# Four score bands in one fill and one 2048-column exponential per half-step

## The reference, cut to what matters

```
x0, x1, x2 = einsum('bnc,c->bn', xf, w1|w2|w3) + b       # n = 4096 positions of one image
sim   = x0[:, :, None] * x1[:, None, :]                  # 4096 x 4096
sm    = softmax(sim, axis=1)
feats = einsum('bn,bnm->bm', x2, sm)
gate  = sigmoid(feats);  layer = gate * x
```

## Time and profile before

| | us |
|---|---|
| median of 3 runs | 5597.88 (5597.68 to 5598.18) |
| the profiled execution, its time | 5609.25 |
| the profiled execution, its span | 5607.3 |
| PE busy | 5256.8 (94%) |
| DVE busy | 4116.6 (73%) |
| ACT busy | 3974.4 (71%) |
| POOL busy | 1925.3 (34%) |

### The profile page before, as it was taken

How to read it: one execution, slowest core, us unless ns; L and a number is a source line. 1 busy time by engine, 2 the same in 40 slices (tenths; PEclk the granted TensorE clock), 3 DMA queues, 4 the chain that set the end, 5 groups by cost and what they waited for, 6 DMA issues and landing times.

```text
span 5607.3 us, 113930 instructions
## 1 busy us (share of the span) xinstructions
PE 5256.8 (94%) x44520; PEld 2738.1 (49%) x44520; DVE 4116.6 (73%) x8686; ACT 3974.4 (71%) x6017; POOL 1925.3 (34%) x1588
## 2 busy tenths in 40 slices
PE   7799999999999999999999999999999999999996
PEld 3436445364553645446364553645446364453624
DVE  8467677777777777677777777777777776777726
ACT  1467868677785877868677785877858678676795
POOL 3224243342423424243341423424234251433403
PEclk9899999999999999999999999999999999999997
DMA  2010201102011020201102011020201102011000
GB/s 85 6 40 11 67 26 50 38 6 72 20 61 31 17 64 14 66 26 39 47 7 71 22 61 31 13 67 14 64 28 32 52 11 67 26 45 41 7 31 31
DMA packets 163252, 211.22 MB, mean 38 GB/s; under 512 B 13216, under 2 KB 146080, under 8 KB 162720
## 3 DMA queue, kind: packets, MB, share of 16 engines
q1 hardware_dynamic: 138144, 136.79, 7.6%
q0 software_dynamic: 24576, 67.14, 4.1%
HBM read 136.78 MB, written 67.11 MB: 36 GB/s over the span
## 4 chain that ended last, share of the span: by engine, by line
PE 67%; ACT 13%; DVE 11%; issue 6%; POOL 2%; DMA 1%; ACTq 0%; DVEq 0%; POOLq 0%; SPq 0%
PE PS L1185 33%; PE PS L1362 15%; PE PS L1353 6%; ACT n_x L510 3%; DVE stats L839 2%; PE PS L1461 2%; PE PS L1219 2%; PE PS L1243 2%; PE PS L1296 2%; ACT xin L510 2%; ACT big L582 2%; ACT work L549 1%; ACT attn L559 1%; ACT soft L582 1%; DMA quant_H<-emb_t,idx 1%
## 5 line engine op out<-in xcount | busy, mean ns | idle before, releaser
L582 ACT ACTIVATE big<-PS 128x1024 f32<-128x1024 f32 x1376 | 1365.8, 1024 | 463.5 <-PE PS L1353 401.8
L582 ACT ACTIVATE soft<-PS 128x1024 f32<-128x1024 f32 x672 | 676.1, 1024 | 352.9 <-PE PS L1353 345.2
L405 POOL DMA_INDIRECT quant_H<-emb_t,idx x512 | 487.5, 952 | 979.9 <-DVE idx L863 788.2
L1185 PE MATMUL PS<-e_hi,n_hi 128*128 128x512 f16 x2048 | 781.4, 382 | 17.5 <-POOL n_lo L398 8.5
L1185 PE MATMUL PS<-e_lo,n_hi 128*128 128x512 f16 x2048 | 778.0, 380 | 0.0
L1185 PE MATMUL PS<-e_hi,n_lo 128*128 128x512 f16 x2048 | 777.8, 380 | 0.0
L1362 PE MATMUL PS<-big,w 128*4 128x512 f32 x5504 | 756.8, 639 | 0.0
L839 DVE BATCH_NORM_STATS2 stats<-XT 128x6 f32<-128x512 f32 x1024 | 651.8, 683 | 14.5 <-POOL XT L421 4.9
L863 DVE FIND_INDEX8 idx<-m,work 128x8 uint32<-128x1024 f32 x512 | 622.1, 1219 | 0.0
L1353 PE MATMUL PS<-rhs,lhs 12*128 12x512 bf16 x4096 | 558.3, 395 | 60.9 <-ACT big L582 38.6
L857 DVE CUSTOM_DVE_ANT_0 work<-PS,e_bias,m 128x512 f32<-128x512 f32 x512 | 384.0, 750 | 211.7 <-PE PS L1185 205.8
(11 more groups left out here) (208 smaller groups left out, 10795.1 us busy)
## 6 DMA issues: line engine op xcount, KB each, us to landing
xin<-x SPq DMA_DIRECT2D x128, 512.0 KB, 3.9
out<-yout SPq DMA_DIRECT2D x128, 512.0 KB, 2.9
quant_H<-emb_t,idx POOLq DMA_INDIRECT x512, 2.7
XT<-emb SPq DMA_DIRECT2D x1, 1024.0 KB, 6.1
XT<-wh SPq DMA_DIRECT2D x1, 256.0 KB, 5.7
XT<-wqv SPq DMA_DIRECT2D x1, 256.0 KB, 5.8
XT<-wk SPq DMA_DIRECT2D x1, 128.0 KB, 5.7
w_sb<-w SPq DMA_DIRECT2D x1, 128.0 KB, 5.3
```

Source lines behind the costliest of these rows:

```text
L405: nc.gpsimd.indirect_dma_start(quant[:, g % 2, u, :], None, emb_t, bass.IndirectOffsetOnAxis(ap=idx[:, t % (2 * GT), 0:1], axis=0),).then_ ...
L582: nc.scalar.activation(E[h % 3][:, z * 1024:(z + 1) * 1024], bank(2 * z, 2), ACT.Exp).then_inc(exped.sem, 1)
L1185: ins = mm(dst, a, b, start=first and j == 0, stop=last and j == 2)
```

## The change

`whole(im, h)` is true for half-steps 1 to 63 of images 0 to 14. There `fill(im, h, 0)` does nothing, and `fill(im, h, 1)` writes all four bands with four matmuls. It waits, as line 1350 has it, until both exponential counts of half-step `h-1` are reached. `exp(im, h, 0)` is then one exponential of 2048 columns, and `exp(im, h, 1)` does nothing. Half-step 0 and the last image keep the old form. The order of the stretch in the 15 rounds of the loop is written anew on POOL, ACT, DVE and PE. The tail and what follows the stretch are the same work in the same order. The calls `prepare(new, ...)` that the new lists hold do nothing for `new` > 0.

The core of the diff, with the new order of PE over the stretch, and of ACT at its beginning and around half-step 32:

```diff
@@ -290,6 +290,9 @@
 
         def z_ps(im, c):
             return bank(0 if im == B - 1 and c % 2 == 1 else 5).rearrange("p (u n) -> p u n", u=2)
+
+        def whole(im, h):
+            return h > 0 and im < B - 1
 
         def back_bank(im, c):
             return 4 if im == B - 1 and c % 2 == 1 else 6
...
             def exp(im, h, z):
-                act.wait_ge(*filled.after(im, 2 * h + z))
+                if whole(im, h):
+                    if z == 1:
+                        return
+                    act.wait_ge(*filled.after(im, 2 * h + 1))
+                else:
+                    act.wait_ge(*filled.after(im, 2 * h + z))
                 if z == 0:
                     act.wait_ge(*summed.room(im, h, 3))
                     if h == 2 and im > 0:
                         act.wait_ge(*l3_ctxed.after(im - 1, NG - 1))
-                nc.scalar.activation(E[h % 3][:, z * 1024:(z + 1) * 1024], bank(2 * z, 2),
-                                     ACT.Exp).then_inc(exped.sem, 1)
+                if whole(im, h):
+                    nc.scalar.activation(E[h % 3], bank(0, 4), ACT.Exp).then_inc(exped.sem, 2)
+                else:
+                    nc.scalar.activation(E[h % 3][:, z * 1024:(z + 1) * 1024], bank(2 * z, 2),
+                                         ACT.Exp).then_inc(exped.sem, 1)
 
...
             def fill(im, h, z):
                 f, t = h // NT, h % NT
+                if whole(im, h) and z == 0:
+                    return
                 if h + z == 0:
                     pe.wait_ge(*pieces_kept[0].after(im, 2))
                     pe.wait_ge(*pieces_kept[1].after(im, 1))
@@ -1348,10 +1362,10 @@
                 if h == 0 and z == 1 and im > 0:
                     pe.wait_ge(*l3_qlo.after(im - 1, NG - 3))
                 pe.wait_ge(*exped.room(im, 2 * h + z, 2))
-                for r in range(2 * z, 2 * z + 2):
+                for r in range(0 if whole(im, h) else 2 * z, 2 * z + 2):
                     rr = slice(32 * r, 32 * r + PIECES)
                     ins = mm(bank(r), lhs[rr, t * P:(t + 1) * P], rhs[rr, f * GW:(f + 1) * GW], start=True, stop=True)
-                ins.then_inc(filled.sem, 1)
+                ins.then_inc(filled.sem, 2 if whole(im, h) else 1)
 
             def sums(im, h):
                 f, t = h // NT, h % NT
@@ -1497,103 +1511,101 @@
             gn(new, 2, 2); project(new); extremes(new); piece_turn(new, 0); piece_turn(new, 1); piece_turn(new, 2)
             piece_turn(new, 3); piece_turn(new, 4)
             for new, old, last in images(B):
-                l3_kturn(last, 7); fill(old, 0, 0); fill(old, 0, 1); fill(old, 1, 0); fill(old, 1, 1)
...
```

New order on ACT (block `scalar`), beginning and half-steps 31 to 36:

```diff
+                exp(old, 0, 0); exp(old, 0, 1); exp(old, 1, 0); exp(old, 1, 1); combine(last, 0); exp(old, 2, 0)
+                exp(old, 2, 1); exp(old, 3, 0); exp(old, 3, 1); l3_qexp(last, 7); exp(old, 4, 0)
+                l3_qturn(last, 6); exp(old, 4, 1); exp(old, 5, 0); final_sq(last, 0); exp(old, 5, 1)
+                exp(old, 6, 0); exp(old, 6, 1); exp(old, 7, 0); exp(old, 7, 1); final_sq(last, 1); exp(old, 8, 0)
+                exp(old, 8, 1); exp(old, 9, 0); l3_qturn(last, 7); final_sq(last, 2); exp(old, 9, 1)
+                exp(old, 10, 0); final_sq(last, 3); exp(old, 10, 1); exp(old, 11, 0); final_sq(last, 4)
...
+                exp(old, 31, 0); exp(old, 31, 1); l0_norm(new, 0, 0); l0_norm(new, 0, 1); l0_norm(new, 0, 2)
+                l0_norm(new, 0, 3); exp(old, 32, 0); l0_norm(new, 1, 0); l0_norm(new, 1, 1); l0_norm(new, 1, 2)
+                exp(old, 32, 1); l0_norm(new, 1, 3); l0_norm(new, 2, 0); l0_norm(new, 2, 1); exp(old, 33, 0)
+                exp(old, 33, 1); exp(old, 34, 0); exp(old, 34, 1); l0_norm(new, 2, 2); l0_norm(new, 2, 3)
+                exp(old, 35, 0); exp(old, 35, 1); exp(old, 36, 0); exp(old, 36, 1); exp(old, 37, 0)
+                l0_norm(new, 3, 0); l0_norm(new, 3, 1); exp(old, 37, 1); exp(old, 38, 0); exp(old, 38, 1)
...
```

New order on PE (block `tensor`), the whole stretch. `fill(old, h, 0)` with `h` > 0 is empty:

```diff
+                fill(old, 0, 0); fill(old, 0, 1); l3_kturn(last, 7); fill(old, 1, 0); fill(old, 1, 1)
+                fill(old, 2, 0); sums(old, 0)
+                l3_ctx(last, 7); fill(old, 2, 1); fill(old, 3, 0); sums(old, 1)
+                fill(old, 3, 1); l3_qturn(last, 6); combine(last, 1); combine(last, 2); fill(old, 4, 0)
+                fill(old, 4, 1); fill(old, 5, 0); sums(old, 2)
+                final_z(last, 0); fill(old, 5, 1); fill(old, 6, 0); sums(old, 3)
+                sums(old, 4)
+                fill(old, 6, 1); fill(old, 7, 0); l3_qturn(last, 7); final_z(last, 1); fill(old, 7, 1)
+                fill(old, 8, 0); final_out(last, 0); sums(old, 5)
+                fill(old, 8, 1); fill(old, 9, 0); final_z(last, 2); fill(old, 9, 1); sums(old, 7)
+                final_out(last, 1); sums(old, 8)
+                fill(old, 10, 0); fill(old, 10, 1); turn_in(new, 0); fill(old, 11, 0); final_z(last, 3)
+                fill(old, 11, 1); sums(old, 9)
+                final_out(last, 2); final_z(last, 4); turn_in(new, 1); fill(old, 12, 0); fill(old, 12, 1)
+                fill(old, 13, 0); final_z(last, 5); sums(old, 10)
+                fill(old, 13, 1); fill(old, 14, 0); final_out(last, 3); turn_in(new, 2); final_z(last, 6)
+                fill(old, 14, 1); sums(old, 11)
+                sums(old, 12)
+                final_z(last, 7); fill(old, 15, 0); turn_in(new, 3); final_out(last, 4); fill(old, 15, 1)
+                fill(old, 16, 0); sums(old, 13)
+                fill(old, 16, 1); final_out(last, 5); fill(old, 17, 0); turn_in(new, 4); sums(old, 14)
+                sums(old, 15)
+                final_out(last, 6); fill(old, 17, 1); turn_in(new, 5); fill(old, 18, 0); final_z(last, 8)
+                prepare(new, 0); fill(old, 18, 1); fill(old, 19, 0); final_out(last, 7); sums(old, 16)
+                final_z(last, 9); sums(old, 17)
+                fill(old, 19, 1); turn_in(new, 6); final_z(last, 10); turn_in(new, 7); fill(old, 20, 0)
+                final_out(last, 8); final_z(last, 11); fill(old, 20, 1); fill(old, 21, 0); final_out(last, 9)
+                turn_in(new, 8); final_z(last, 12); fill(old, 21, 1); fill(old, 22, 0); sums(old, 19)
+                turn_in(new, 9); sums(old, 20)
+                final_out(last, 10); fill(old, 22, 1); sums(old, 21)
+                final_z(last, 13); turn_in(new, 10); final_out(last, 11); fill(old, 23, 0); fill(old, 23, 1)
+                final_z(last, 14); fill(old, 24, 0); fill(old, 24, 1); sums(old, 23)
+                turn_in(new, 11); final_out(last, 12); fill(old, 25, 0); fill(old, 25, 1); fill(old, 26, 0)
+                final_z(last, 15); sums(old, 24)
+                final_out(last, 13); turn_in(new, 12); fill(old, 26, 1); fill(old, 27, 0); sums(old, 25)
+                final_out(last, 14); fill(old, 27, 1); turn_in(new, 13); turn_in(new, 14); fill(old, 28, 0)
+                fill(old, 28, 1); final_out(last, 15); sums(old, 26)
+                fill(old, 29, 0); fill(old, 29, 1); turn_in(new, 15); sums(old, 27)
+                fill(old, 30, 0); fill(old, 30, 1); fill(old, 31, 0); sums(old, 28)
+                gn(new, 0, 1); gn(new, 0, 2); fill(old, 31, 1); fill(old, 32, 0); fill(old, 32, 1); sums(old, 29)
+                score(new, 0, 0); score(new, 0, 1); score(new, 1, 0); score(new, 1, 1); fill(old, 33, 0)
+                fill(old, 33, 1); score(new, 2, 0); fill(old, 34, 0); sums(old, 32)
+                fill(old, 34, 1); score(new, 2, 1); score(new, 3, 0); fill(old, 35, 0); fill(old, 35, 1)
+                sums(old, 33)
+                score(new, 3, 1); score(new, 4, 0); turn0(new, 0); score(new, 4, 1); sums(old, 34)
+                score(new, 5, 0); fill(old, 36, 0); fill(old, 36, 1); score(new, 5, 1); score(new, 6, 0)
+                fill(old, 37, 0); fill(old, 37, 1); sums(old, 35)
+                fill(old, 38, 0); turn0(new, 1); score(new, 6, 1); score(new, 7, 0); fill(old, 38, 1)
+                sums(old, 36)
+                score(new, 7, 1); fill(old, 39, 0); fill(old, 39, 1); fill(old, 40, 0); score(new, 8, 0)
+                score(new, 8, 1); fill(old, 40, 1); sums(old, 37)
+                fill(old, 41, 0); sums(old, 38)
+                turn0(new, 2); sums(old, 39)
+                score(new, 9, 0); score(new, 9, 1); score(new, 10, 0); fill(old, 41, 1); score(new, 10, 1)
+                fill(old, 42, 0); fill(old, 42, 1); fill(old, 43, 0); turn0(new, 3); score(new, 11, 0)
+                fill(old, 43, 1); score(new, 11, 1); score(new, 12, 0); sums(old, 40)
+                score(new, 12, 1); turn0(new, 4); score(new, 13, 0); fill(old, 44, 0); score(new, 13, 1)
+                fill(old, 44, 1); score(new, 14, 0); score(new, 14, 1); turn0(new, 5); fill(old, 45, 0)
+                score(new, 15, 0); score(new, 15, 1); score(new, 16, 0); score(new, 16, 1); score(new, 17, 0)
+                turn0(new, 6); fill(old, 45, 1); sums(old, 42)
+                score(new, 17, 1); sums(old, 44)
```

(69 more changed lines are left out.)

245 lines of the change are left out of this document (91 added, 154 removed).

## The result

The changed kernel took 5874.62 us (median of 4 runs, 5864.6 to 5882.28), the kernel before 5598.03 us beside it. The ratio is 1.0484, with a 95% interval of 1.0472 to 1.0496. It is slower by 277 us, 18.4 us for each of the 15 rounds. The forecast was 5780 us, 12 us a round, and its range ended at 5910. The profiled execution took 5882.28 us.

What follows compares the result with a forecast made beforehand. ACT and PE were taken to bound the first half by turns, PE the second. Lost overlap +8.3 us a round plus 4 of other waits gave +12, 15 rounds 180 us: 5780 us, range 5690 to 5910 (chance 0.75).

Steps and rivals of the forecast that it cites:

- The exponential: ACT's exponential of 2048 columns, which no row showed: taken as 1.88 us, with bounds 1.72 and 1.95 us.
- The link: From a four-band fill's start to its exponential's start: 0.43 us, part of a least half-step of 2.36 us.
- The second half: Half-steps 32 to 63 of a round: PE's work 136.3 us, longer sums 145.8, nine steps short by 9.5 us.
- the longer of the two sums, nothing lent: Each half-step costs the longer of PE's work and ACT's chain; what one lacks cannot come from the next step.
- The first half: Half-steps 0 to 31 of a round, 82.3 us before: 2.0 us for step 0 plus 84.1 for steps 1 to 31.
- my 15.4 us: Time PE is made to wait in half-steps 1 to 31, where 21 steps hold too little PE work.
- The 15 us of waits: Old stretch's waits, for exponentials and for DVE's copies, group norm and POOL: 222.6 us less 208 us of PE work.
- rival C: Pile-up: PE's waits delay scores and final_z, DVE and POOL run late; +21 us a round, 5913 us, chance 0.15.
- The clock: PE's clock, 0.97 in the last image's second half, would not drop; at 0.88 some 6 us more.
- POOL: l0_norm(new, 2, 3) now before index(new, 2): costed at nothing, or 5.2 us a round if the cover fails.
- Rival A: A saving: fewer, larger exponentials relieve ACT and the new order covers each gap; 4 us a round, 5540 us, chance 0.07.
- Rival B: No change from 5598 us: forced waits replace the old ones and a third of the forced 24.9 us vanishes; chance 0.03.

Runs made afterwards that it cites:

- the third corner: Kernel before with its old order lists, but four-band fills and each whole half-step's exponential halved to 1024 of 2048 columns: 5722.16 us, 1.0206.

## Why the prediction was right, and what was mis-sized

- *The exponential.* 1.88 us, as taken.
- *The link.* I took 0.43 us from fill to exponential. It is 0.49, and 0.71 at the half clock. The four matmuls of that row were two fills, and the exponential began on its own pair, so the row was too short. A step takes 2.43, not 2.36 us. That is 0.07 x 30 steps = 2 us a round.
- *The second half.* Forecast 145.8 - 1.0 = 144.8 us with the sums behind the end taken off, measured 143.7. The sum agrees, its parts do not: PE's marked waits for exponentials are 2.7 us where I counted 9.5, and all its idle time there is 5.9 us (3.3 before). So the agreement is partly luck, and it does not show the rule "the longer of the two sums, nothing lent".
- *The first half.* Forecast 2.0 + 84.1 = 86 us and a share of 4 for other waits, measured 98.7. This term failed. The direct wait is even smaller than my 15.4 us (7.3 of marked waits), and the other waits were not what the old stretch had: its waits for DVE are 1.0 us, the new ones 10.5. I had taken the old waits as staying, with 4 us a round for them, and had priced no chain but that of fill and exponential. The 15 us of waits that I took from the prices of the old list are not in the earlier trace rows either: PE's idle time there is 3.0 and 3.3 us.
- *The range.* 18.4 us a round is above the +6 to +18 that got the chance of 0.75. The time lies in the range only because its upper end took in half of rival C, so this part is luck. (The 2 us between 15 x 12 = 180 and the 182 in the sum have no row.)

Where the new waits come from shows in the timeline. Before:

```profile
1631.68 0.27 PE L1185 MATMUL PS<-m_hi,n_x 128*128 128x256 f16 x1
...
1631.99 0.38 ACT L648 ACTIVATE o_hi<-PS 128x256 f32<-128x256 f32 x1
```

After:

```profile
1695.75 0.27 PE L1197 MATMUL PS<-m_hi,n_x 128*128 128x256 f16 x1
...
1696.34 0.39 PE L1367 MATMUL PS<-rhs,lhs 12*128 12x512 bf16 x4 [0.32 <-ACT big L591]
...
1696.83 1.88 ACT L591 ACTIVATE big<-PS 128x2048 f32<-128x2048 f32 x1 [0.55 <-PE PS L1367]
...
1698.61 0.38 ACT L659 ACTIVATE o_hi<-PS 128x256 f32<-128x256 f32 x1
...
1699.57 0.69 DVE L1052 TENSOR_TENSOR soft<-PS,gamma_b 128x512 f32<-128x512 f32 x1 [4.44 <-ACT o_hi L659]
...
1700.32 0.28 PE L1197 MATMUL PS<-m_hi,quant_H 128*128 128x256 f16 x1 [0.84 <-DVE soft L1052]
```

Before, `final_sq` began 0.3 us after the start of the last matmul of its `final_z`. After, it stands in ACT's list behind an exponential, which waits for a fill, which waits for the exponential before. It began 2.9 us after that start, 2.6 us after its data were there. DVE came after it, then the bank of `final_z` was free, and PE had waited 0.84 us. That is rival C's mechanism, at the place that the forecast costed with 4 us. It is shown by the third corner for the old order (6.1 us with halved, 11.5 us with full exponentials).

For the new order it explains little. The row has 3.4 of the 10.5 us there, in five waits, and only two of them (0.30 and 0.84 us) stand behind a late `final_sq`. The longest is this:

```profile
1709.26 0.27 PE L1197 MATMUL PS<-m_hi,n_x 128*128 128x256 f16 x1
...
1709.56 0.38 ACT L659 ACTIVATE o_hi<-PS 128x256 f32<-128x256 f32 x1
...
1710.51 0.69 DVE L1052 TENSOR_TENSOR soft<-PS,gamma_b 128x512 f32<-128x512 f32 x1
...
1711.25 0.28 PE L1197 MATMUL PS<-m_hi,quant_H 128*128 128x256 f16 x1 [0.96 <-DVE soft L1052]
```

Here `final_sq` began at once, and the ring from PE over ACT and DVE back to PE took 2.0 us all the same. The new list has only a `turn_in` and a fill between these two `final_z`, where the old one had a `sums` and another fill besides, so PE was back too early. This fits the two kernels in which the waits for DVE did not shrink: 11.4 us with halved exponentials and 10.9 us with the overlap put back. That the places in PE's list make them is not tested, so the cause of most of these 10.5 us stays open. The others (`final_out` and `turn_in` behind each other's DVE copies, and the chain from `l3_ctx` to `combine` at the stretch's start) are read from the waits and no run isolates them.

- *The clock.* "I expect no drop" was wrong: 0.96 to 0.91 in the first half, 0.88 to 0.80 in image 0. I had judged by the last image, where the waits are short. A mean of 0.91 between the two levels is 18% of 98.7 us at 1.2 GHz, 18 us, against 8% of 82.3, 7 us. The 11 us more can cost at most half of themselves, 5 to 6 us a round, an estimate and the figure that I had kept for the upper part.
- *Image 0.* Forecast 77.7, measured 91.7 us. Steps at the half clock take 2.65 us (257.69 to 260.34), and two `sums` in a step then outlast the exponential: one took 1.89 us (at 255.59) where it takes 1.04 at the full clock.
- *POOL.* The wait for ACT's conversions did not grow: 8.1 us in 3 waits in the second half, against 26.1 in 5. As far as these rows show, costing the move at nothing was right.
- *The rest.* 115.3 against 115.0 us. ACT's idle time in the first half is 98.7 - 76.0 = 22.7 us, above the 12 named.
- *Rival A* is refuted by size: the large exponential saves under 10 us a kernel, if anything. *Rival B* is refuted by the 277 us.

No version here that computes every exponential beats the kernel before. ACT's exponentials are worth little in that one: without half of them it is 1.3% faster.

## What to carry to other kernels

Before you merge two turns of a buffer into one, look for what else stands in the consumer's queue: the wait that you add to it delays every instruction behind it and comes back to the producer by other banks. Price every ring in which engines hand a bank round, not only the one that you change, and compare it with the work that stands between two turns: 2.0 us for the bank of `final_z`, 2.43 us for the exponentials here. Price it from release to next start, and let a row give it only if its instruction waited for the very matmul that the row ends with. An order written out by hand belongs to one pattern of waits: here each of the two parts alone was slower than both together, so don't judge either alone.

## What the hardware showed unasked

A fill of two bands and one of four keep PE equally long (0.32 us until the next instruction), so merging two fills that already stood together saves nothing. At the half clock the path from a fill's start to its exponential grew from 0.49 to 0.71 us, as much as the fill itself (0.40 to 0.61). And halving the exponentials of the kernel before, which took ACT's work in the first half from 75.5 to 51.4 us, shortened that half by 2.8 us.
